# A graph network's setup on VectorE: 49 unrolled row counts and 49 unrolled layernorm statistics written as two loops of seven turns

## What is computed

```python
h = jnp.maximum(_layernorm(x, axis=-1), 0.0)
x = x + _L0_gnn_ref(h, edge_index, L0_gnn_W1, L0_gnn_b1, L0_gnn_W2, L0_gnn_b2)   # two convolutions
h = jnp.maximum(_layernorm(x, axis=-1), 0.0)
x = x + _L1_gnn_ref(h, edge_index, edge_attr_64, L1_gnn_u, batch0, ...)          # segment sum and MLP
...
deg = jax.ops.segment_sum(jnp.ones_like(dst, dtype=x.dtype), dst, num_segments=N)
dis = jax.lax.rsqrt(jnp.maximum(deg, 1.0))
norm = dis[src] * dis[dst]
```

## Time and profile before

| | us |
|---|---|
| median of 3 runs | 1436.68 (1434.59 to 1437.53) |
| the profiled execution, its own time | 1436.67 |
| its span, first to last instruction | 1435.0 |
| DVE busy in the span | 886.2 (62%) |
| PE busy in the span | 1133.5 (79%) |

### The profile page before, as it was taken

The page is one execution under the profiler, slowest core; times in us unless marked ns, Lnnn a source line. Parts: engine busy times, 40 slices in busy tenths (PEclk is TensorE's granted clock), DMA queues, the critical chain, the costliest instruction groups (busy, mean ns, idle before and its releaser), DMA issues. The chain is left out here.

```text
span 1435.0 us, 31864 instructions
## 1 busy us (share of the span) xinstructions
PE 1133.5 (79%) x10325; PEld 749.0 (52%) x10325; DVE 886.2 (62%) x1543; ACT 484.0 (34%) x1067; POOL 203.8 (14%) x170
## 2 busy tenths in 40 slices
PE   0012089999925889999999998549999999999974
PEld 0001089999924566666666664224444444444443
DVE  7575698888828979999999991621222222222221
ACT  0024100000006778888888882410111111111111
POOL 5710610000013922111111000300000000000000
PEclk9999999999966989999999999759999999999975
DMA  8423379999820545665446665959477777777400
GB/s 192 149 68 98 94 232 288 286 285 283 262 58 14 187 142 197 219 218 181 163 167 219 211 200 185 318 180 345 140 227 232 231 229 228 234 224 228 112 14 11
DMA packets 231891, 270.89 MB, mean 189 GB/s; under 512 B 31003, under 2 KB 202565, under 8 KB 231662
## 3 DMA queue, kind: packets, MB, share of 16 engines
q1 hardware_dynamic: 137258, 173.78, 39.5%
q10 hardware_dynamic: 89904, 81.89, 17.2%
q0 software_dynamic: 4688, 14.70, 3.3%
HBM read 178.73 MB, written 91.61 MB: 188 GB/s over the span
## 5 line engine op out<-in xcount | busy, mean ns | idle before, releaser
L779 ACT CAST adj_all<-win_p 128x392 f32 x784 | 346.9, 497 | 44.7 <-PE win_p L829 22.9
L829 PEld LDWEIGHTS win_p<-mv,st 128*128 128x128 f16 x3136 | 213.4, 100 | 141.8 <-ACT adj_all L779 21.7
L829 PE MATMUL win_p<-mv,st 128*128 128x98 f16 x3136 | 256.2, 211 | 17.9 <-ACT adj_all L779 10.7
L727 DVE TENSOR_TENSOR st<-iota_lo,code 128x2048 f16 x196 | 241.2, 1230 | 32.8 <-ACT code L768 13.2
L1369 PE MATMUL dense_p_b<-adj_all,g_hi 128*128 128x512 f16 (+1 forms) x637 | 232.2, 372 | 18.7 <-SPq L1127 16.6
L543 PE MATMUL agg_p<-ahot,arows 128*64 128x64 f32 x3724 | 218.8, 223 | 34.5 <-DVE ahot L584 34.5
L844 PE MATMUL dense_p<-adj_all,g_hi 128*128 128x448 f16 x686 | 241.5, 352 | 1.2 <-DVE total L738 0.8
L844 PE MATMUL dense_p<-adj_all,g_lo 128*128 128x448 f16 x686 | 242.1, 353 | 0.0
L543 PEld LDWEIGHTS agg_p<-ahot,arows 128*64 128x64 f32 x3724 | 218.7, 139 | 34.6 <-DVE ahot L584 34.6
L1369 PE MATMUL dense_p_b<-adj_all,g_lo 128*128 128x512 f16 (+1 forms) x637 | 232.1, 371 | 0.0
L727 DVE TENSOR_TENSOR mv<-iota_mv,code 128x1568 f16 x196 | 190.8, 973 | 0.0
(11 more groups left out here) (162 smaller groups left out, 1017.6 us busy)
## 6 DMA issues: line engine op xcount, KB each, us to landing
adj_d<-adj_all ACTq DMA_DIRECT2D x14, 5488.0 KB, 19.4
adj_all<-adj_d SPq DMA_DIRECT2D x11, 6272.0 KB, 23.5
arows<-in_edge_attr_dram SPq DMA_DIRECT2D x98, 608.0 KB, 3.6
adj_all<-adj_d SPq DMA_DIRECT2D x7, 896.0 KB, 9.9
disb<-dis_d SPq DMA_DIRECT2D x24, 256.0 KB, 4.9
hT_d<-hT ACTq DMA_DIRECT2D x12, 256.0 KB, 2.8
cur<-hT_d SPq DMA_DIRECT2D x12, 256.0 KB, 7.5
h1T_d<-total SPq DMA_DIRECT2D x12, 256.0 KB, 6.5
```

The source lines that it names most:

```text
L727: ins = nc.vector.tensor_tensor(hot[:, bass.ds((b * BG + j) % 2, 1), u, :, :] .rearrange("p a w (n t) -> p (a w) n t", t=2), iota[:, :].re ...
L779: nc.scalar.copy(adj[:, bass.ds(b % 2, 1), :, bass.ds(j * GN + k * WN, WN)] .rearrange("p b h d -> p (b h) d"), win_p[:, k % 4, 0:WP * MV] ...
L829: ins = nc.tensor.matmul(win_p[:, k % 4, 0:WP * MV] .rearrange("p (h c t) -> p h c t", c=WP, t=PN)[:, :, c, :], st[:, odd, k // UW, pair, ...
```

## The change

The row counts and the `bn_stats` stand each in a `Fori` of HI // SB = 7 turns with seven blocks in the body. The block number is then `b * SB + k` with b in a register, and the addresses of the tiles are computed from it. The waits of the row counts become `gate`s on new semaphores (`s_counted`, `s_row_f`) with register values; the statistics count `s_stats`. The recounts stay unrolled and get a semaphore of their own, `s_recounted`, since `s_dve` is no longer counted in between.

```diff
-                for k in range(HI):
-                    ch.reuse(k, 4)
-                    ch.step(nc.vector.tensor_scalar(cmp[:, k % 4, 0:NSR], heads_b[:, :], tgt[:, k:k + 1], None,
-                                                    ALU.is_lt, ALU.add, accum_out=cnt[:, k:k + 1]))
-                    if k % SB == SB - 1:
-                        ks = slice(k + 1 - SB, k + 1)
-                        ch.wait()
-                        ch.link(nc.vector.tensor_scalar(cnt[:, ks], cnt[:, ks], -1.0, 0.0, ALU.add, ALU.max))
-                        nc.vector.tensor_copy(row_i[:, ks], cnt[:, ks]).then_inc(s_rows_i, 1)
+                with dve.Fori(0, HI // SB) as b:
+                    for k in range(SB):
+                        if k >= 4:
+                            gate(dve, s_counted, b * SB + (k - 3))
+                        nc.vector.tensor_scalar(cmp[:, k % 4, :], heads_b[:, :], tgt[:, bass.ds(b * SB + k, 1)], None,
+                                                ALU.is_lt, ALU.add, accum_out=cnt[:, bass.ds(b * SB + k, 1)]
+                                                ).then_inc(s_counted, 1)
+                    ks = bass.ds(b * SB, SB)
+                    gate(dve, s_counted, b * SB + SB)
+                    nc.vector.tensor_scalar(cnt[:, ks], cnt[:, ks], -1.0, 0.0, ALU.add, ALU.max).then_inc(s_row_f, 1)
+                    gate(dve, s_row_f, b + 1)
+                    nc.vector.tensor_copy(row_i[:, ks], cnt[:, ks]).then_inc(s_rows_i, 1)
 
                 dve.wait_ge(s_x, 32)
-                for k in range(HI):
-                    ch.step(nc.vector.bn_stats(stats[:, k, :], h[:, k, :]))
-                ch.wait()
+                with dve.Fori(0, HI // SB) as b:
+                    for k in range(SB):
+                        nc.vector.bn_stats(stats[:, bass.ds(b * SB + k, 1), :].rearrange("p a s -> p (a s)"),
+                                           h[:, bass.ds(b * SB + k, 1), :].rearrange("p a f -> p (a f)")
+                                           ).then_inc(s_stats, 1)
+                dve.wait_ge(s_stats, HI)
...
-                    ch.reuse(k, 4)
-                    ch.step(nc.vector.tensor_scalar(cmp[:, k % 4, 0:SR], rows[:, k, :], tgt[:, k:k + 1], None,
-                                                    ALU.is_lt, ALU.add, accum_out=cnt2[:, k:k + 1]))
-                ch.wait()
+                    if k >= 4:
+                        dve.wait_ge(s_recounted, k - 3)
+                    nc.vector.tensor_scalar(cmp[:, k % 4, 0:SR], rows[:, k, :], tgt[:, k:k + 1], None,
+                                            ALU.is_lt, ALU.add, accum_out=cnt2[:, k:k + 1]).then_inc(s_recounted, 1)
+                dve.wait_ge(s_recounted, HI)
```

More of the change, by code:

```diff
@@ L236, in build @@
             s_heads_f = sem("s_heads_f", ph)
+            s_counted = sem("s_counted", ph)
+            s_row_f = sem("s_row_f", ph)
+            s_stats = sem("s_stats", ph)
+            s_recounted = sem("s_recounted", ph)
             block = ph.enter_context(nc.Block())
```

## The result

| | before | changed |
|---|---|---|
| median of 20 runs each, alternating on one chip, us | 1434.49 (1429.87 to 1440.97) | 1438.21 (1435.23 to 1443.10) |
| profiled execution, its own time / span, us | 1436.67 / 1435.0 | 1438.16 / 1436.4 |
| `shift` starts, us | 94.61 | 99.27 |

The ratio of the times is 1.003, 95% interval [1.0019, 1.0041]: 3.7 us or 0.26% slower, where 11.2 us were forecast. The size was wrong, and the next rows show that this was no mere rounding of a term. In the experiments three runs of the kernel before (1512, 1847 and 6500 us) lie far above all others, and the ratios leave them out.

A forecast was written before the change was run, and what follows sets the result against it. DVE's statistics leading to `shift` were taken to bound the setup. Later row counts, a slow stretch lasting to 88.1 us and looped statistics moved their end from 89.25 to 100.4: 1436.67 + 11.2 = 1448 us, range 1419 to 1458.

The forecast's parts named there:

- The bound and the path: Setup, first phase: its end is set by DVE's chain through the statistics, `bn_aggr` and `shift`.
- The factor of 1: From `shift` to the kernel's end: whatever moves the statistics' end moves these by as much, in both directions.
- the spell: Slow stretch on DVE from about 49.8 to 84.12 us, costing some 28 us; forecast to belong to POOL's gathers and stay.
- The turn: DVE's row counts: a loop turn adds 0.6 us (bounds 0.3 and 1.2), so seven take 6.50 us instead of 5.90.
- `bn_stats` in the loop: DVE's statistics outside the slow stretch: 0.29 us each plus 0.6 per turn; the 32 left take 9.3 and 3.0 us.
- gates pay too: Rival, DVE's slow stretch: gates and register instructions also pay its price; +20 us, 1456 us, chance 0.12.
- The wait of 9.04 us: DVE's wait for all seven counts, ahead of L331 in the last turn: carried over unchanged, ending at 70.4 us.
- The forecast's own explanation: DVE's slow stretch: each finished instruction that raises a semaphore must clear it or its record through something the gathers crowd.
- The step that failed: POOL's last seven gathers start late, end 3.6 to 4.0 us later, and DVE's slow stretch with them, at 88.1 us.
- The signs of being wrong: DVE: `bn_stats` at 0.3 us from the start, or a short wait ahead of L331 in the last turn.
- Rival C: DVE's setup: the slow stretch belongs to the unrolled code and goes with it; 15.9 us earlier, 1421 us, chance 0.36.
- rival T: DVE's setup, named only in the experiments: the slow stretch belongs to a time or place in the program; no chance given.

The follow-up runs named there:

- e5: The changed kernel (both loops) run again on another chip, against the kernel before: 1414.71 us, ratio 1.0044.
- e6: The unrolled kernel before, unchanged, run again for its profile, against an identical kernel: 1406.63 us, ratio 0.9979.
- e2: Only the statistics put in a loop, row counts left unrolled, against the kernel before: 1411.38 us, ratio 1.0015.
- e8c: The kernel before with an iota and a wait on POOL behind every gather: a single run, 1463.51 us beside 1431.57 us for the kernel before.

## Why the prediction was wrong

**The bound and the path** were right. `shift` sets the end of the setup, and its 4.7 us reached the next phase whole in the recorded pair. The factor of 1 is not general: without the spell 10.3 us at `shift` became 7.1 us (e5 against e6).

**The turn** of the row counts was right: 0.6 forecast, 0.67 to 0.70 measured. The Trainium skill, "Advanced Engine Details and Errata", section "Control Flow Timing", gives 108 ns for a compare-and-branch. The timeline has no row for a branch, but the trace of e5 has records: the branch itself lasts 0.05 to 0.06 us, and when it is taken the next record starts 0.19 to 0.22 us (counts) or 0.27 to 0.34 us (statistics) behind its start, against 0.10 when it is not taken. The turn with its gates is six times the page's figure, so that figure alone would have sized the change far too small. The Trainium skill, "Runtime: NRT & Kernel Launch", section "Instruction fetch mechanics", warns of a fetch at a taken branch outside the resident window; the queue has one instruction packet in 50 to 90 us where the two loops take six branches in that stretch, and no turn is long beside it. So no branch of these loops waited for a fetch in the trace.

**`bn_stats` in the loop** was over-sized outside the spell: forecast 7 x 0.29 + 0.6 = 2.63 us a turn, measured 2.10 (e5), or 1.90 where the counts were unrolled (e2). Inside a turn they are (1.81 - 0.29) / 6 = 0.25 apart, and the turn adds 0.34, where 0.6 was taken over from the other loop. For the 49 this is 14.9 us instead of the 17.8 that 49 x 0.29 + 6 x 0.6 would give. Why the same loop is 0.2 us a turn slower behind the counts' loop is not explained.

**The price inside the spell** was mis-stated: "gates pay too" stood among the rivals with 0.12, and it is what happened. A compare with a gate took 2.80 us and not 2.10, and the short operations of a turn 4.1 and 4.2. Yet the row indices came at 76.9, between the forecast's 71.8 and that rival's 78.8 or so (its statistics were to start at 79.6, and they started at 77.4), since the first four compares of a turn paid only 1.40, while the sixth turn was caught by the spell too. The wait of 9.04 us that the forecast carried over did not come back: ahead of L331 stand 2.01 us in the sixth turn and 0.16 in the last. The forecast's own explanation, a price for each finished instruction that raises a semaphore, does not hold either, for address and branch instructions, which raise none, pay the same (the records are in the last section).

**The step that failed** is "so the gathers end 3.6 to 4.0 us later, and with them the spell: 84.1 + 4.0 = 88.1". I had the spell tied to the last gather. But I had also worked out, in the same paragraph, that POOL would run dry before its last seven gathers, and did not ask what a pause would do to a thing that the gathers feed. The trace shows it: POOL issues nothing from 69.5 to 77.3, the last slow interval ends at 75.44, and the statistics, forecast at 28.0 us, took 16.6. Against the forecast they start 5.0 us later (77.4, not 72.4) and last 11.4 us less, which is the 6.5 us by which `bn_aggr` came earlier than its 100.4. Against the kernel before, 9.5 of the 14.1 us that the late indices cost are repaid. That the sign came out right is partly luck, since two misses of opposite sign met. So the late indices did harm and good: they delayed the statistics and moved them out of the spell. That the spell ended before 77.4 is shown; that POOL's pause ended it is argued.

**The signs of being wrong** both came: `bn_stats` ran at 0.25 to 0.3 from the start, and the wait ahead of L331 in the last turn was short. By the prediction's own words the spell would then be of the code's form. The rows deny that conclusion, since the loops have the spell from 47.44 to 75.44; the signs did not tell a spell that is gone from one that ends early.

**Rival C**, the spell goes with the unrolled code, is out: the changed kernel has the spell in the recorded pair and the unrolled one has none in e6. The loops neither make nor cure it. But its price list was nearly the loops' true one without a spell, where they cost 10.3 us at `shift`.

**What stays open:** what, if anything, fills up, why the spell shows in all 40 recorded runs' times and in none of the experiments' profiles, and whether POOL's pause is its cause of ending or stands beside it by chance. For the pause speak the one trace of the changed kernel and e8c; the runs that were to decide it did not meet the spell. Two rivals stand untested. A spell of a set length would fit nearly as well, with 34 us of late rows before the change (about 50 to 84.12) and 28 after it (47.44 to 75.44). And by rival T the end could hang on a time or place, though it fell at different times and at different code in the two traces.

## What to carry to other kernels

Idle time that is put down to "issue" or "remote" on an engine with nothing to wait for may belong to a state of the chip: see whether it is there on a second chip before a change is priced by it. Here 25 us of 1435 came and went that way, more than any edit but the slowed gathers moved.

When a change makes one engine late, ask for each queue that it feeds what a pause of that queue ends, not only what it delays.

On DVE a turn of seven row counts cost 0.67 to 0.70 us more in a loop than unrolled, of which 0.3 stand idle ahead of the first compare and 0.2 behind the gate of L333. A turn of seven `bn_stats` cost 0.5 (e2) to 0.7 us (e5) more: some 0.3 for the turn itself, and the rest because with two register instructions ahead they come 0.23 to 0.25 us apart instead of 0.195. The fourteen turns together are 10.3 us at `shift`, worth unrolling where the setup sets the critical path. Where ACT is idle, 49 squares there and one reduce in place of 98 short instructions on DVE gained more than either form.

## What was unexpected of the hardware

The trace of the changed kernel also records DVE's register operations, waits and branches. From 43.1 to 75.4 us 23 of them last 0.69 to 0.71 us each, where they last 0.02 to 0.12 in e5, and nearly all start 1.40 us behind the one before. A single one more stands at 86.4, in the one long turn of the statistics. Counting them at 1.40 gives the prices above: an ungated compare has one, a gated one two (2.80), and three stand between L331 and L333 (4.10) and again behind it (4.22). In the earlier trace rows `bn_stats` came at the same 1.40.

In the same stretch landings of gathers are missing from the trace. Between 50 and 80 us the kernel before records 31, where e6 has 319 and e5, whose gathers then keep their full pace nearly to the end, 368. The shortage begins long before DVE is late: between 25 and 30 us 51 are recorded, where e6 has 110, and the first late DVE row comes at about 50. In the changed kernel the last seven gathers, behind the pause, have 49 of their 112 again. Whether the landings themselves or only their records were missing is not shown; the data of the gathers moved as always, 2352 packets in every one of these profiles. The gathers kept their pace of 1.26 us throughout, so nothing on POOL's rows betrays the spell.

The first late DVE row stood 34 us behind the first gather before the change (15.79 to about 50) and 30 us in the changed kernel (17.00 to 47.44). With gathers at less than half the rate (e8c) it had not come when the statistics ended, 45 us behind the first gather.
